# Identity products without a reader on TensorE, at the head of each norm and around the start of the small heads' pipeline

## The reference

```python
x = x + 0.5 * L0_ffn(layernorm(x))     # 512x512 matrix, a rank-32 adapter, 8 gates
x = x + L0_attn(layernorm(x))          # 32 heads of 16 channels, causal, rotary, 10 adapter tokens
x = x + 0.5 * L0_ffn(layernorm(x))
x = x + 0.5 * L1_ffn(layernorm(x))     # mixture of 16 experts, 2 a token, and a shared one
x = x + L1_attn(layernorm(x))          # 32 query heads of 128 channels, 8 key/value heads
x = x + 0.5 * L1_ffn(layernorm(x))
```

## Time and profile before

| | |
|---|---|
| median of 3 runs | 1802.05 us (1801.62 to 1803.87) |
| the profiled execution | 1799.84 us |
| its span | 1798.1 us |
| mean granted TensorE clock | 0.946 |
| PE busy | 1606.9 us, 89% of the span |
| PE weight loads busy | 1242.7 us, 69% |
| DVE, ACT, POOL busy | 1004.5, 900.9, 984.8 us |

### The profile page before, as it was taken

How to read it: one execution, slowest core, us unless ns; L and a number is a source line. 1 busy time by engine, 2 the same in 40 slices (tenths; PEclk the granted TensorE clock), 3 DMA queues, 4 the chain that set the end, 5 groups by cost and what they waited for, 6 DMA issues and landing times. The chain is left out here.

```text
span 1798.1 us, 26487 instructions
## 1 busy us (share of the span) xinstructions
PE 1606.9 (89%) x8164; PEld 1242.7 (69%) x8164; DVE 1004.5 (56%) x2630; ACT 900.9 (50%) x1876; POOL 984.8 (55%) x1122
## 2 busy tenths in 40 slices
PE   5597899998768998589999999999999999979996
PEld 4486555546547886467878788787878778757884
DVE  5561556551657236655656565656565656665235
ACT  3112565652221231477777776777677777731230
POOL 2252555541221443378787877777878777812533
PEclk9798789988879999899999999999999999989999
DMA  2200000000134933244544353444434344463834
GB/s 85 91 10 3 2 3 2 3 3 1 37 141 154 339 133 111 85 107 108 115 111 114 82 136 89 107 108 103 122 91 127 81 100 89 91 229 121 318 119 139
DMA packets 312096, 180.24 MB, mean 100 GB/s; under 512 B 281895, under 2 KB 283767, under 8 KB 309568
## 3 DMA queue, kind: packets, MB, share of 16 engines
q1 hardware_dynamic: 300160, 152.81, 30.5%
q0 software_dynamic: 11840, 26.25, 4.7%
HBM read 111.08 MB, written 22.54 MB: 74 GB/s over the span
## 5 line engine op out<-in xcount | busy, mean ns | idle before, releaser
L1325 POOL TENSOR_TENSOR st_prob<-st_prob,st_rinv 128x512 f32<-128x512 f32 x256 | 266.3, 1040 | 177.0 <-DVE st_rinv L1393 177.0
L1329 POOL TENSOR_TENSOR st_plane<-st_prob,st_plane 128x512 f16<-128x512 f32 x256 | 307.6, 1211 | 0.3 <-ACT st_plane L1245 0.3
L1245 ACT ACTIVATE st_plane<-st_prob 128x512 f16<-128x512 f32 x256 | 161.2, 630 | 126.9 <-POOL st_prob L1325 126.8
L1261 ACT ACTIVATE st_prob<-st_score,st_nmax 128x512 f32<-128x512 f32 x256 | 175.2, 685 | 59.8 <-DVE st_nmax L1400 57.2
L1400 DVE TENSOR_REDUCE st_nmax<-st_score 128x1 f32<-128x512 f32 x256 | 175.1, 684 | 41.5 <-PE st_score L108 38.6
L2038 DVE CUSTOM_DVE_ANT_0 st1b_dump<-st1b_score,st1b_maskrow 128x128 f32<-128x128 f32 (+3 forms) x256 | 112.7, 487 | 95.5 <-PE st1b_score L1736 68.9
L1240 ACT ACTIVATE st_pthi<-st_plane_t 128x512 fp32r<-128x512 f16 x256 | 159.5, 623 | 3.4 <-DMA st_plane_t<-st_plane 3.2
L1370 DVE CAST st_ptlo<-st_plane_t 128x512 fp32r<-128x512 f16 x256 | 148.9, 582 | 2.6 <-DMA st_plane_t<-st_plane 2.6
L1374 DVE TENSOR_TENSOR st_olo<-st_outp,st_ohi 128x512 fp32r<-128x512 f32 x64 | 44.2, 690 | 166.8 <-ACT st_ohi L1249 166.8
L1893 ACT ACTIVATE st1b_slabs<-st1b_across 128x512 f32<-128x512 f32 (+1 forms) x192 | 90.6, 526 | 90.4 <-PE st1b_across L1755 70.1
L106 PE MATMUL st_outp<-st_pthi,st_vhi 128*128 128x512 f32 x256 | 103.8, 406 | 28.4 <-ACT st_pthi L1240 27.4
(11 more groups left out here) (380 smaller groups left out, 4056.3 us busy)
## 6 DMA issues: line engine op xcount, KB each, us to landing
st_raw<-in_moe_w SPq DMA_DIRECT2D x40, 768.0 KB, 7.3
sorted_outs<-st_ln_xn SPq DMA_DIRECT2D x62, 256.0 KB, 4.1
st_qraw<-in_gqa_q SPq DMA_DIRECT2D x8, 1024.0 KB, 5.4
st_oraw<-in_gqa_o SPq DMA_DIRECT2D x8, 1024.0 KB, 5.3
rows<-st_ln_xn SPq DMA_DIRECT2D x2, 2048.0 KB, 9.3
st_kvraw<-in_gqa_kv SPq DMA_DIRECT2D x8, 512.0 KB, 3.9
st_plane_t<-st_plane SPq DMA_TRANSPOSE x256, 2.7
st1a_raw<-in_w_attn SPq DMA_DIRECT2D x3, 1024.0 KB, 6.6
```

What stands on the lines that cost most here:

```text
L1245: act.activation(plane[t][:, 0:T], prob[:, t, :], ACT.Copy).then_inc(upper_ready, 1)
L1261: act.activation(prob[:, t, :], score[t][:, :], ACT.Exp, bias=nmax[:, slot:slot + 1], accum_out=rsum[:, slot:slot + 1]).then_inc(exp_ready, 1)
L1325: pool.tensor_tensor(prob[:, t, :], prob[:, t, :], rinv[:, slot:slot + 1].broadcast_to([P, T]), ALU.mult).then_inc(norm_ready, 1)
L1329: pool.tensor_tensor(plane[t][:, T:2 * T], prob[:, t, :], plane[t][:, 0:T], ALU.subtract).then_inc(lower_ready, 1)
```

## The change

A helper `warm` issues n products of the identity with itself into the first 128 columns of a bank. Nothing waits for them and nothing reads them, and they signal no semaphore. It is called with n = 40 at the head of `Norm.tensor` (six norms, into the last of the norm's banks), with n = 10 ahead of the wait for `ake_step`, with n = 6 behind the signal `aket_ready` and ahead of the wait for `akt_ready`, and with n = 2 at the end of each of the six parts of turns -3 and -2 (into `across[0]`).

```diff
+def warm(pe, bank, ident, n):
+    for _ in range(n):
+        pe.matmul(bank[:, 0:P], ident[:, :], ident[:, :], start=True, stop=True)
...
     def tensor(self, pe):
+        warm(pe, self.bank[-1], self.ident, 40)
         for n, (h, k) in enumerate(self.order):
             pe.wait_ge(self.xn_ready, TB * (h + 1))
             for t in range(TB):
...
                             if u.has():
                                 values(u, 0, 1)
-
+                        if u.unit() < -1:
+                            warm(pe, across[0], ident, 2)
+
+                warm(pe, across[0], ident, 10)
                 wait(pe, ake_step, 4)
                 for n in range(NG0 * PAIRS):
                     last = pe.transpose(misc[:, n * 2 * AK:(n + 1) * 2 * AK], ake[:, 2 * n:2 * n + 2, :, :].rearrange("p n s d -> p (n s d)"),
                                         ident[0:2 * AK, 0:2 * AK])
                 last.then_inc(aket_ready, 1)
+                warm(pe, across[0], ident, 6)
                 wait(pe, akt_ready, 1)
                 wait(pe, cleared, NCLEAR)
                 pipeline(turn)
```

## The result

The changed kernel takes **1812.78 us**, the median of 20 runs (1803.31 to 1819.16), beside 1802.18 us for the kernel before in 20 runs (1796.38 to 1810.21). The ratio is 1.0052, with an interval of [1.0037, 1.0068]: slower by 6.7 to 12.3 us. The forecast was 1804.8, from 1799.5 to 1809.5, so the sign that it held second likeliest came out, and the time lies above its range.

A forecast was written before the change was run, and what follows sets the result against it. TensorE, busy 89% of the span, was taken as the bound, with its half-clock work to be won. Terms 3.1 - 1.5 - 0.4 + 2.7 - 0.3 + 0 - 0.8 = +2.8 us on 1802.05 gave 1804.8 us, range 1799.5 to 1809.5.

The forecast's parts named there:

- the sign that it held second likeliest: Whole kernel: slower, chance 0.37, behind same at 0.53 and ahead of faster at 0.10.
- The new waits in st0 and st2: Norms of st0 and st2: the 80 records end after the rows are ready, +3.1 and +2.7 us.
- st1a: Norm of st1a: transposes run warm and DVE's differences then set the first product, -1.5 us.
- the small heads' term: Fill of the small heads: a late start, mostly recovered through turn -1, together -0.4 us.
- The delay: Small heads: 36 records ahead of q's first transpose make the first scores 2.35 us late.
- The recovery up to turn -1: Small heads, first scores to turn -1: 3.7 us instead of 5.42, a gain of 1.7 us.
- The recovery in turn -1: Small heads, turn -1: first part at full clock, the rest as before, a gain of 1.0 us.
- Turns 1 to 15 and the projection as unchanged: Behind the fill of the small heads: no term in the sum for the steady turns or the projection.
- Rival 1: Small heads: products carry the clock through turns -1 and 0, -5 us there, 1798 in all; chance 0.10.
- Rival 2: Small heads, turn -1: clock falls again before the delay is recovered, 1807.6 us; chance with its mixtures 0.33.
- Rival 3: All added products: they do not lift the clock, 40 cost 17.2 us everywhere, well over 1830 us; chance 0.02.
- rival 4: Norms: transposes do not hold the clock the products gave, about +13 us, 1815; chance 0.02.

The follow-up runs named there:

- e1_norms: The changed kernel without the products in the small heads, keeping the 40 at all six norms; 1805.06 us, ratio 1.0019 to the kernel before.
- e2_heads: The changed kernel without the 40 at the norms, keeping the small heads' 10, 6 and 2s; 1806.17 us, ratio 1.0031 to the kernel before.
- e7_through: e2_heads without the 6, its 2s in turns -2 and -1 instead of -3 and -2; 1796.40 us, ratio 0.9966 to the kernel before.
- e9_steady: The kernel before plus only seven products in a PE wait in nine steady turns; 1794.93 us, ratio 0.9969 to the kernel before.

## Why the prediction was wrong, point by point

**The norms were about right.** The price of the 80 records was forecast at 8.9 us warm and 11.0 from cold; it was 9.17 warm (st4 and st5), 10.80 in st1a and st2, and 11.37 in st0. The new waits in st0 and st2 were forecast at +3.1 and +2.7; st0 gave +3.1 in this pair and +2.5 between the means of all profiles with and without products there, and st2 +2.6 once the late load is set aside. st1a came to -1.6 in this pair and -1.2 between the means (forecast -1.5), through the path that was named: the transposes warm, DVE the bound. st3 gave +0.2 (-0.3), st4 -0.3 (0), with the clock lost in the gap, st5 -0.7 (-0.8). All six together: +3.4 us measured by e1_norms [-0.5, +7.4], +3.2 forecast.

**The failed step is the small heads' term: -0.4 forecast, +5.6 us measured (+2.5 to +8.8).** Within it:

- *The delay* was named rightly and put a little low. First scores +2.35 forecast; +3.3 in the changed kernel, +2.4, +3.9 and +2.4 in the three profiles of e2_heads' program (mean +3.0). The clock fell behind the small adapter transposes as assumed (at 171.5 in the changed kernel), and the 36 records took 5.9 us for 5.7.
- *The recovery up to turn -1* was mis-sized: 1.7 us forecast, 0.85 measured (4.6 us from the first scores to turn -1 in all four profiles, 5.4 before, 3.7 forecast). The forecast halved all of PE's own work. The transposes did halve, but the two score products with 512 columns took 1.10 us at full clock (180.60 in the changed kernel) and 1.37 at half (175.93 before).
- *The recovery in turn -1* came as forecast, its first part at full clock and the rest at half, and was a little larger: 1.3 to 1.6 us for 1.0. At turn 0 the kernels with the change's products are 0.1 to 1.5 us late (mean 0.7) where 0.4 early was forecast, and at turn 1 0.9 late on the mean of the four. All that stands ahead of turn 1 thus explains 1.3 of the missing 6.0 us.
- *Turns 1 to 15 and the projection as unchanged* was the step that failed: a term put at nothing, without a bound. Turns 1 to 15 are 200 us of unchanged instructions, and in the profiles with no added product inside them they took from 195.8 to 208.4 us. A forecast that touches their start had to carry that spread in its range. By the means of four and five profiles, +3.1 us of the term lie in these turns and +1.8 in the projection behind them. The twelve runs of e2_heads show that its loss is more than the late start of turn 1. That the fill makes these stretches slow, and how, stays open: the spread of the turns is three times the difference, and one of the four profiles (199.8) is against it.

**What the comparison of two profiles added** to this: 2.8 us of a late load in st2, and the 2.3 us by which the profiled execution of before lay under its median. The forecast also put instruction fetch at nothing. The page counts 101 packets of instruction loads after the change and 96 before; no kernel with added code and no added products was run, so their share is not known. The signs of the parts cannot be read from one profile each; e1 and e2 with twelve runs each could tell them.

**The rivals.** Rival 1 (the fill stays warm) was false for this change, and its place right: e7_through, with the products in turns -2 and -1, keeps the clock through most of turn 0 and gains 0.34%. Rival 2 had the place of the fall right, turn -1, but not its condition: 2.2 to 2.4 us of the delay were recovered by turn 0 (2.7 forecast), more than the 1.9 under which that rival was to decide. Its 1807.6 would have been nearer to the 1812.8, for another reason than the one it gives. Rival 3 is excluded (80 records from cold took 10.8 and 11.4 us, not 17.2). So is rival 4: st0's 32 transposes took 3.66 us behind the products, where that rival had 6.9, and the clock also rose on the norms' own transposes in the kernel before. The Trainium skill ("TensorE: Matmul & The Clock Gate", Part 4, PE-mode transpose) says that the full clock does not engage for transpose-mode work, as it does not count as busy in the same way. For these float32 transposes the trace does not agree: the clock rose at 89.5 us behind 5.0 us of them alone.

## What to carry to other kernels

Unread products are free only if they end before the work behind them is ready: measure that wait (2.8 us in st0) against their price at both clocks (8.9 and 17.2 us), and put them where PE waits inside a pipeline that already runs, not ahead of a chain that has yet to start (e7_through and e9_steady gain 0.3% each, the change lost 0.5%). Neither a higher mean clock nor a busier PE says that they help, since the products fill both. Where unchanged work behind the edit runs at a clock that varies from one execution to the next, bound it in the forecast, and judge by a dozen runs a side and never by one profile.

## What was not expected of the hardware

- Identical instructions took 197.0 to 207.5 us in five profiles without products in the heads, and 199.8 to 208.4 in three profiles of e2_heads' program. The time goes with the granted clock of the stretch, 0.94 at 197.0 and 0.88 at 208.4. The clock fell there after very different stretches at full clock: in the changed kernel at 212.5 us, after 3.40 us with PE busy for 1.73, and in the kernel before at 273.8, after 3.40 us with PE busy for all of them:

```profile
270.40:273.80 3.40, 3.40 (x30) 2.78 (x34) 1.23 (x9) 1.89 (x6) 1.45 (x6) 1.00 0.01 2
273.80:277.20 3.40, 3.40 (x20) 1.86 (x13) 2.62 (x9) 1.39 (x3) 1.62 (x5) 0.50 0.00 1
```

- The spread of the kernel before goes with its clock: of its 35 runs beside e1_norms, the five fastest took 1794.9 to 1795.7 us at a mean granted clock of 0.946 to 0.948, the five slowest 1808.1 to 1810.9 at 0.938 to 0.940.
- Across kernels the same number misleads: 0.962 at 1812.7 us for the changed kernel, 0.946 at 1799.8 for the one before.
- The load of 1088 KB in st2 landed after 7.9 us instead of 5.1 in one execution, with the same issues in the same order around it. The load of 1 KB just ahead of it took 3.5 us instead of 1.6, and the DMA view of that stretch counts one instruction load that the kernel before does not have there. What delayed it was not tried.
